# The gathers of the expert results add to the residual in the DMA, in two stages of a transformer block kernel on one Trainium2 core

## What is computed

```python
x = x + 0.5 * moe_ffn(layernorm(x))         # top 1 of 4 experts, inner 1024, gelu, layernorm with gamma and beta
x = x + attention(layernorm(x))             # 16 heads of 16, causal softmax
x = x + 0.5 * moe_ffn(layernorm(x))         # the same weights again
x = x + 0.5 * fp4_ffn(layernorm(x))         # inner 704, inputs and weights rounded blockwise to fp4
x = x + linear_attention(layernorm(x))
x = x + 0.5 * fp4_ffn(layernorm(x))
```

## Time and profile before

| | |
|---|---|
| Median of 3 runs | 2492.87 us (2490.41 to 2495.44) |
| The profiled execution, its own time | 2492.54 us |
| Its span, first to last instruction | 2490.8 us |
| Busy: PE, DVE, ACT, POOL | 2109.1, 1547.7, 970.3, 982.3 us |
| Mean granted clock of PE | 0.949 of full speed |

### The profile page before, as it was taken

How to read it: one execution, slowest core, us unless ns; L and a number is a source line. 1 busy time by engine, 2 the same in 40 slices (tenths; PEclk the granted TensorE clock), 3 DMA queues, 4 the chain that set the end, 5 groups by cost and what they waited for, 6 DMA issues and landing times. The chain is left out here.

```text
span 2490.8 us, 40519 instructions
## 1 busy us (share of the span) xinstructions
PE 2109.1 (85%) x12456; PEld 1313.4 (53%) x12457; DVE 1547.7 (62%) x3843; ACT 970.3 (39%) x1883; POOL 982.3 (39%) x1249
## 2 busy tenths in 40 slices
PE   5359999596999999986399995798998999689996
PEld 3236666352444444445166664566665666456664
DVE  4213333567888888837433333899966666489994
ACT  1012223141666666652132221333325666533331
POOL 4412222761111111124512223666546666455553
PEclk9999999796999999998599998899998999899999
DMA  7111111345433333120211112000000000000002
GB/s 282 44 49 46 49 46 45 91 152 101 60 58 53 53 52 52 27 104 9 74 37 46 48 46 72 22 15 15 4 1 2 2 2 2 1 1 1 0 0 68
DMA packets 88634, 114.08 MB, mean 46 GB/s; under 512 B 13488, under 2 KB 69040, under 8 KB 88368
## 3 DMA queue, kind: packets, MB, share of 16 engines
q1 hardware_dynamic: 82352, 95.53, 15.6%
q0 software_dynamic: 6144, 16.79, 2.1%
HBM read 73.08 MB, written 38.93 MB: 45 GB/s over the span
## 5 line engine op out<-in xcount | busy, mean ns | idle before, releaser
L1022 DVE TENSOR_REDUCE a_part_max<-a_psS 128x1 f32<-128x512 f32 (+3 forms) x608 | 362.4, 653 | 76.5 <-PE a_psS L950 67.8
L1078 ACT ACTIVATE a_PT<-a_psE 128x512 f32<-128x512 f32 (+1 forms) x608 | 309.3, 583 | 188.9 <-PE a_psE L964 171.9
L944 PE MATMUL a_psS<-a_sk,a_sq 96*128 96x512 bf16 (+3 forms) x768 | 234.4, 341 | 23.5 <-DMA a_sk<-qk_parts 19.7
L523 PE MATMUL e_psY<-wo_moe,e_gT 128*128 128x256 f32 x1120 | 253.0, 379 | 0.0
L557 DVE TENSOR_TENSOR e_hb<-e_psH,b 128x1024 f32<-128x1024 f32 x70 | 85.7, 1224 | 267.8 <-PE e_psH L508 209.7
L925 POOL TENSOR_SCALAR_AFFINE_SELECT a_PT<-a_PT 128x512 f32<-128x512 f32 x128 | 81.5, 636 | 419.0 <-ACT a_PT L1078 419.0
L583 POOL TENSOR_TENSOR e_rstd<-e_moments,minus_half 128x1 f32<-128x1 f32 x70 | 42.8, 611 | 476.0 <-DVE e_moments L121 476.0
L964 PE MATMUL a_psE<-a_sq,a_sk 98*128 98x512 bf16 (+3 forms) x768 | 224.5, 329 | 2.5 <-ACT a_PT L1078 1.4
L540 ACT ACTIVATE e_g<-e_hb 128x1024 f32<-128x1024 f32 x70 | 74.0, 1057 | 384.9 <-DVE e_hb L557 384.9
L523 PEld LDWEIGHTS e_psY<-wo_moe,e_gT 128*128 128x128 f32 x1120 | 207.5, 190 | 25.4
L1363 POOL TENSOR_TENSOR f_hv<-f_hv,f_hm 128x704 f32<-128x704 f32 x64 | 100.3, 1566 | 239.8 <-DVE f_hv L1139 239.8
(11 more groups left out here) (272 smaller groups left out, 4237.2 us busy)
## 6 DMA issues: line engine op xcount, KB each, us to landing
a_sq<-qk_parts SPq DMA_DIRECT2D x96, 128.0 KB, 4.2
a_sk<-qk_parts SPq DMA_DIRECT2D x96, 128.0 KB, 6.7
e_xs<-sorted_x SPq DMA_DIRECT2D x70, 128.0 KB, 2.0
e_xr<-sorted_x SPq DMA_DIRECT2D x70, 128.0 KB, 2.0
sorted_y<-e_yo SPq DMA_DIRECT2D x70, 128.0 KB, 1.7
sorted_x<-zeros SPq DMA_DIRECT2D x1, 4480.0 KB, 23.6
X<-x_in SPq DMA_DIRECT2D x4, 1024.0 KB, 9.7
w<-w_in SPq DMA_DIRECT2D x1, 4096.0 KB, 22.3
```

The lines of the kernel that those rows point to most:

```text
L523: mm = pe.matmul(psY[p][:, 0:D], gT[p][:, k, :], st.wo_moe[:, k, :], start=k == 0, stop=k == KI - 1)
L944: mm = pe.matmul(out[:, i * n:(i + 1) * n], sq[it % 3][0:SROWS, h0 + i, qt * P:(qt + 1) * P], sk[it % 3][0:SROWS, h0 + i, c * 512:c * 512 ...
L1022: dve.tensor_reduce(part_max[:, c, h0:h0 + heads, qt], psS[place % RING][:, 0:heads * n].rearrange("p (h k) -> p h k", h=heads), AX.X, ALU ...
L1078: act.activation(PT[kt % 2][:, h0:h0 + heads, q0:q0 + n], psE[e % RING][:, 0:heads * n].rearrange("p (h q) -> p h q", h=heads), ACT.Exp, s ...
```

## The change

The indirect DMA gets an operation: it reads the destination row of `X`, adds the row of `sorted_y` and writes the sum to `X`. Its target is `X` itself. DVE's additions (line 659, 8 of them, and line 1289, 16 of them) go, with the wait behind each, and the semaphore `joined`. The buffer `gathered` of the q stage is no longer allocated. The number, order and place of the gathers in POOL's program, the relays and all waits for `arrived` stay as they are.

```diff
     def start(self, pool, g):
         for t in range(g * self.group, (g + 1) * self.group):
-            pool.indirect_dma_start(self.st.gathered[:, t, :], None, self.st.sorted_y[:, :],
-                                    bass.IndirectOffsetOnAxis(ap=self.st.slot[:, t:t + 1], axis=0)
-                                    ).then_inc(self.landed[g % 2], 16)
+            pool.indirect_dma_start(self.st.X[:, t, :], None, self.st.sorted_y[:, :],
+                                    bass.IndirectOffsetOnAxis(ap=self.st.slot[:, t:t + 1], axis=0),
+                                    compute_op=ALU.add).then_inc(self.landed[g % 2], 16)
...
-    MOMENTS = 4
+    MOMENTS = 3
...
                 dve.wait_ge(gather.arrived, (g + 1) * G)
                 reuse(dve, normed, g, G)
-                tiles = st.X[:, bass.ds(g * G, G), :]
-                c.link(dve.tensor_tensor(tiles, st.gathered[:, bass.ds(g * G, G), :], tiles, ALU.add))
                 dve.memset(c.pause, 0.0)
...
-    gather, joined = (Gather(st, sem, tag, 2), sem(tag + "joined")) if gathers else (None, None)
+    gather = Gather(st, sem, tag, 2) if gathers else None
...
                 if gathers:
                     dve.wait_ge(gather.arrived, t + 2)
-                    pair = st.X[:, bass.ds(t, 2), :]
-                    dve.tensor_tensor(pair, pair, st.gathered[:, bass.ds(t, 2), :], ALU.add).then_inc(joined, 2)
-                    dve.wait_ge(joined, t + 2)
                 take_moments_of_pair(dve, c, st.X, t, stats[i], moments[i], LN_EPS)
...
-        with nc.sbuf_tensor("gathered", [P, TILES, D], F32) as st.gathered:
-            run(qkv_phase, "q_")
+        run(qkv_phase, "q_")
...
-        st.gathered = st.V
         run(fp4_ffn_phase, "f0_", True)
```

## The result

The changed kernel takes 2495.39 us, median of 14 runs (2492.71 to 2502.79); the kernel before, run beside it, 2491.00 us (2489.55 to 2495.44). The ratio is 1.0021, 95% interval 1.0011 to 1.0030: slower by 0.2%, where 2486.0 us and a gain of 0.3% had been forecast. The time lies inside the stated range (2482 to 2499), but outside the forecast's own (2482 to 2488) and on the other side of the kernel before. The profiled execution of the changed kernel took 2502.0 us, near the top of its runs, so its stages tell more than its total.

A forecast was written before the change was run, and what follows sets the result against it. DVE was taken to bound `f0_`, and POOL's gathers, then PE's stream, the q stage. The terms 0 - 8.3 + 1.0 + 0.5 = -6.8 us against 2492.5 gave 2485.7, as a median 2486.0 us; range 2482 to 2499.

The forecast's parts named there:

- x: Growth of one gather's descriptor work on POOL from the addition; bounded by 0 and 0.95 us, taken as 0.05.
- Part 3: Longer gathers on POOL, at the q stage's start, behind it and at the start of `f0_`: +1.0 us.
- the prediction's own formula: q stage pays 16x + max(0, 16x - 4.4); whole change 20x + max(0, 16x - 4.4) - 7.8.
- rival 1: POOL's gathers become the bound in the q stage: slower, 2498 at x = 0.48, 2515 at 0.95; chance 0.20.
- The rule against the change: A reduction in a DMA issues two read descriptors per chunk, a copy one; by it x would be about 0.48.
- Part 1: q stage: eight additions taken off DVE, covered by POOL's queue and then PE's stream; gain 0.
- Part 2: `f0_`: sixteen additions taken off DVE, eleven counted at 0.75 us each, five early ones at nothing; -8.3 us.
- Rival 3: Another engine, PE or POOL, takes over in `f0_`, so half the gain is lost: 2490; chance 0.11.
- The slack of 4.4 us: q stage: group 5's first tile ready at 519.8, PE turns it at 524.2; POOL's lateness up to this is free.
- Part 4: Later landing of gathers with an addition: covered in the q stage, uncovered at the start of `f0_`; +0.5 us.
- the 4x: Start of `f0_`: four dearer gathers stand before the landing on which everything waits, costing four times x.
- Rival 4: DMA engines set the pace in the q stage and at the start of `f0_`: about 0 gain, 2493; chance 0.07.

The follow-up runs named there:

- q_early_groups: Kernel before, with only groups 0 to 3 of the q stage gathering with the addition in the DMA; 2497.08 us, ratio 1.0022.
- after_parts_on_dve: Changed kernel, with the four last subtractions of a group in the q stage moved from POOL to DVE; 2493.93 us, ratio 1.0013.
- no_additions: Kernel before, gathers plain, with DVE's additions left out in both stages, so expert results of two sublayers are not added; 2481.99 us, ratio 0.9959.
- f0_only: Kernel before, with the addition in the DMA in the first fp4 stage alone, q stage unchanged; 2485.79 us, ratio 0.9981.
- q_late_groups: Kernel before, with only groups 4 to 7 of the q stage gathering with the addition in the DMA; 2494.53 us, ratio 1.0005.
- f0_early_two: Addition in the DMA in the first fp4 stage alone, plus the q stage's first two roots issued ahead of a gather group; 2482.86 us, ratio 0.9965 to before.

## Why the prediction was wrong, point by point

**The step that failed** is the size of x in Part 3. I bounded it by 0 and 0.95 us and took 0.05 from what I called the nearest rows, the scatters. They were near in what they move and far in what the price went with: a scatter and a plain gather have 48 packets each, a gather with an addition 144. Measured: 0.59. With that x the prediction's own formula gives 16 x 0.59 = 9.4 at the start and 9.4 - 4.4 = 5.0 behind it, 14.4 us; the q stage paid 14.1, q_early_groups 8.6 for the first term, and after_parts_on_dve took away the second. What no run separates is the longer descriptor work from the doubled time on the DMA engines at the start of the stage, since every gather with an addition has both; there the rows of POOL by themselves account for the delay (a gather every 1.85 us in place of 1.25, without a wait between). The direction was thus rival 1's, which had a chance of 0.20 and 2498 us at x = 0.48; at 0.59 the formula gives +9. The two stages give +7.5, the profiled execution +9.5, of which 2.5 are the routing with its lower clock, and the medians +4.4 and +7.1; that +9 lies so near +9.5 is chance.

**The rule against the change** deserved more than a sentence. The trace of the changed kernel shows the doubled time of the DMA engines, 0.94 us a gather against 0.46, and 62% more descriptor work on POOL. The Trainium skill's two read descriptors per chunk (Collectives: The Full Stack, The bandwidth ceiling), which that page states for the reduce step of a collective, would have made x about 0.48 by the working of the prediction; the trace agrees with the direction and nearly with the size, 0.59.

**Part 1** held: the additions in the q stage lie beside other work; no_additions left the stage at 127.3.

**Part 2** held in mechanism: -8.3 was forecast, no_additions has -7.9 in the stage, the changed kernel -6.6 and f0_only -5.4. That -7.9 is so near is in part luck. The eleven pairs came down to 183.3 us in the changed kernel, 183.4 in no_additions and 182.6 in f0_only, against 182 forecast; that is 0.6 to 0.7 us a pair, not 0.75, and 5.9 us in no_additions. Its other 1.9 lie ahead of the eleven (61.9 us from the first gather to the first of them, 63.8 before), where the prediction had counted the five early additions at nothing; 62.3 to 63.8 in the traces with plain gathers and additions say how sure that is. The pace of `f1_` was nearly the right comparison. Rival 3 is out.

**Part 3, where it counts**: the route behind the start was another than I gave. I had POOL's lateness reach PE through the normalizing of group 5. PE waited on ACT instead, and ACT on the stores that POOL's last subtraction releases. The slack of 4.4 us came from the wrong pair of rows, and that it gave the right sum is chance; q_late_groups, where PE starts as before, lost 7.6 us behind the start and f0_early_two, where it starts 5.2 us earlier, 2.5, where the formula has 5.0 and 0.8; some of the 7.6 is the stretch at the lower clock.

**Part 4** was taken as +0.5 us and was small: the landing grew from 2.8 to 3.8 us and stayed covered in the q stage. At the start of `f0_` the trace of the changed kernel records no landing, but the wait for it shows: the fifth gather, which waits for the first pair, starts 9.0 to 10.9 us after the first in the seven traces with the addition in the DMA there, and 7.6 to 8.5 in the six with plain gathers. PE's first work came after 22.1 to 23.3 us in those seven, 21.3 to 22.9 in the five with DVE's additions and 21.4 in no_additions. So the 4x (2.4 us at x = 0.59) and the landing together cost 0.7 to 1.9 us against the one trace of no_additions, and the early additions that went hid most of it. Rival 4, with landings of 6 us and more in the q stage, is out.

## What to carry to other kernels

Work that a DMA does in passing need not be free for the engine that writes its descriptors (here 0.59 us a gather): read the price of the issue on that engine's own row, and ask what stands behind it in its queue. An addition taken off an engine pays only where that engine sets the pace; the same edit gave 6.6 us in one stage and cost 14 in the other, so split it by stage before you judge it. When you compare two traces in a fixed window, see that the same instructions fall into it, and look whether a view has a record of the stage at all before you read its maximum. And when the nearest row prices a different operation, keep the whole bracket in the chances, not in the range alone.

## What the runs showed of the hardware

- An indirect DMA of 128 rows of 1 KB with an addition took 1.55 us of descriptor work on POOL against 0.96 us without, 0.94 us of each DMA engine against 0.46, 144 packets against 48, and landed after 3.8 us against 2.8. The landings are those of the q stage. In after_parts_on_dve, with the doubled time on the DMA engines still there, the q stage lost nothing behind its start; the 0.59 us on POOL is what the losses followed.
- Beside the weight loads at the start of `f0_` the first pair of gathers held POOL until 9.0 to 10.9 us after the first gather with an addition (seven traces), and until 7.6 to 8.5 us without (six traces).
- After a stall of PE of 2.8 us in a stretch in which it was busy 6.95 of 10 us, the granted clock fell to the lower level for part of the next 10 us (mean 0.83), and four matmuls took 3.08 us instead of 1.88 (q_late_groups). After a stall of 2.85 us with 6.90 of 10 us busy it stayed at the full level (changed kernel).
- One stage of the same code, the second routing, took 82.7 us with a granted clock of 0.60 and then 1.00 in PE's first two stretches of 7 us, and 85.2 us with 0.50 and 0.55.
